# One opening block instead of two, and another order at the borders of two attentions

## What is computed

```python
x = x + L0_xattn(layernorm(x), ctx, mask)   # 16 heads of 128, 8 key/value heads
x = x + L0_ffn(layernorm(x))                # weights rounded to fp8, silu(gate) * up
x = x + L1_xattn(layernorm(x), ctx)         # 16 heads, queries and keys RMS-normed per head
x = x + L1_ffn(layernorm(x))                # 16 experts, top 2
# xattn: q = xn @ Wq, k = ctx @ Wk, v = ctx @ Wv, softmax(q k / sqrt(128)) v, @ Wo
# RMS norm of q and k: t * rsqrt(mean(t^2) + eps) * g
```

## Time and profile before

| | |
|---|---|
| median of 3 runs | 2272.78 us (2270.73 to 2275.41) |
| the profiled execution | 2273.29 us, span 2271.6 us |
| busy over the span | PE 94%, DVE 68%, ACT 56%, POOL 25% |
| stages in the span, about | opening to 37 us, attention 0 to 766, ffn 0 to 1052, attention 1 to 1946, experts after it |

### The profile page before, as it was taken

One profiled execution on the slowest core, in us unless ns is written; L12 is line 12 of the kernel. 1 busy time (PEld: TensorE's weight loads), 2 busy tenths in 40 slices (PEclk: granted clock), 3 DMA queues, 4 the chain that ended last, 5 costly groups with the idle time before them and its releaser, 6 DMA issues. The chain is left out here.

```text
span 2271.6 us, 38211 instructions
## 1 busy us (share of the span) xinstructions
PE 2137.9 (94%) x12318; PEld 1864.9 (82%) x12318; DVE 1554.3 (68%) x3798; ACT 1260.9 (56%) x3373; POOL 560.4 (25%) x1274
## 2 busy tenths in 40 slices
PE   5999999999999899998999999999999999589993
PEld 4899999999999678887788888888888888378882
DVE  6777777777778884434666666666666667867776
ACT  4555455455454533323666666666666666567772
POOL 1000001001000122223333333333333333144541
PEclk8999999999999999999999999999999999789997
DMA  6122111111210220002111111111111110278886
GB/s 254 65 80 80 46 69 63 61 69 46 78 57 27 70 75 1 1 1 75 47 56 47 56 63 57 46 55 46 55 46 55 58 55 36 83 246 293 291 277 259
DMA packets 74388, 195.83 MB, mean 86 GB/s; under 512 B 8448, under 2 KB 39192, under 8 KB 61488
## 3 DMA queue, kind: packets, MB, share of 16 engines
q1 hardware_dynamic: 64432, 173.60, 21.9%
q0 software_dynamic: 7680, 16.80, 2.2%
q10 hardware_dynamic: 2176, 4.19, 0.5%
HBM read 177.78 MB, written 25.17 MB: 89 GB/s over the span
## 5 line engine op out<-in xcount | busy, mean ns | idle before, releaser
L608 PE MATMUL bank<-l_wkv_hi,l_ctxT 128*128 128x256 f32 (+1 forms) x1024 | 278.8, 344 | 7.0 <-DMA l_ctxT<-ctx_split 5.2
L1025 DVE TENSOR_TENSOR l_v_lo<-bank,l_v_hi 128x128 fp32r<-128x128 f32 (+1 forms) x256 | 91.7, 358 | 213.5 <-ACT l_v_hi L847 212.2
L1025 DVE TENSOR_TENSOR l_pT_lo<-bank,l_pT_hi 128x512 fp32r<-128x512 f32 x256 | 175.2, 684 | 77.9 <-ACT l_pT_hi L872 77.9
L866 ACT ACTIVATE l_probs<-l_scored,l_nbias 128x256 f32<-128x256 f32 x256 | 128.2, 502 | 158.6 <-DVE l_nbias L1078 155.6
L608 PE MATMUL bank<-l_wo_hi,l_oT_hi 128*128 128x512 f32 x512 | 209.3, 409 | 0.7 <-DVE l_oT_lo L1025 0.7
L608 PE MATMUL bank<-xnT_hi,l_wq_hi 128*128 128x512 f32 x512 | 209.8, 410 | 0.0
L608 PEld LDWEIGHTS bank<-l_wkv_hi,l_ctxT 128*128 128x128 f32 x1024 | 183.3, 193 | 28.2 <-issue 6.3
L608 PE MATMUL bank<-xnT_lo,l_wq_hi 128*128 128x512 f32 x512 | 201.7, 394 | 0.0
L608 PE MATMUL bank<-xnT_hi,l_wq_lo 128*128 128x512 f32 x512 | 201.7, 394 | 0.0
L608 PE MATMUL bank<-l_wo_hi,l_oT_lo 128*128 128x512 f32 x512 | 201.1, 393 | 0.0
L608 PE MATMUL bank<-l_wo_lo,l_oT_hi 128*128 128x512 f32 x512 | 200.8, 392 | 0.0
(11 more groups left out here) (288 smaller groups left out, 5949.9 us busy)
## 6 DMA issues: line engine op xcount, KB each, us to landing
l_ctxT<-ctx_split SPq DMA_DIRECT2D x64, 1024.0 KB, 4.8
moe_raw_gu<-in_L_ffn_gate_up_proj SPq DMA_DIRECT2D x32, 1024.0 KB
moe_raw_dn<-in_L_ffn_down_proj SPq DMA_DIRECT2D x32, 512.0 KB
l_raw_a<-in_L_xattn_Wq SPq DMA_DIRECT2D x16, 512.0 KB, 5.8
l_raw_a<-in_L_xattn_Wo SPq DMA_DIRECT2D x16, 512.0 KB, 5.4
x_sb<-in_x SPq DMA_DIRECT2D x4, 1024.0 KB, 11.1
ctx_split<-ct SPq DMA_DIRECT2D x4, 1024.0 KB, 13.6
moe_raw_gu<-moe_y_rows SPq DMA_DIRECT2D x4, 1024.0 KB
```

Of the source, the lines that this page charges most:

```text
L608: mm = nc.tensor.matmul(out, a[x], b[y], start=(i == 0), stop=(i == n - 1))
L866: ins = nc.scalar.activation(probs[u % 2][:, t, :], src, ACT.Exp, bias=nbias[:, i:i + 1], scale=scale, accum_out=rsum[:, i:i + 1])
L1025: nc.vector.tensor_tensor(pair[1], src, pair[0].bitcast(F32), ALU.subtract).then_inc(done, 1)
```

## The change

**Opening.** The two stages become one block, `opening_stage`. DMA order: x group 0, x group 1, both context halves, the weights, x groups 2 and 3. DVE does the layer norm factors of 8 tiles before it touches the context. The normalised rows come from three engines (DVE 1, ACT 4, POOL 3), rows and context groups alternate on PE, ACT and DVE, and rows use four banks in turn. Group 0 of the split context is written straight into `ctxT`, and SP raises `ctx_in` itself, so group 0 isn't loaded back; groups 1 to 3 are kept in parts of `xnT` that are free until later. All four are still stored. In attention 0, SP waits for the four stores before it loads group 1, and ACT before its first `turned_high`.

**Attention borders.** In layer 1's prologue DVE scales the first keys and POOL takes the first query factors; DVE waits for them before the first `biases`. In layer 1's first iteration `split_o` and `split_p` (unit 2) go ahead of `biases` (unit 3). In the last iteration of both layers `copy_p` and `split_p` of unit 0 go ahead of the exponentials of unit 1 and of `statistics`. At the end of layer 1 the statistics of the third group move from the last but one iteration into the last, `take_sums` goes first on DVE, `norm_queries` comes before `late_factors(1)` on POOL, and `normalise(4, 5)` moves behind the exponentials of unit 2.

```diff
+            load_x(0)
+            load_x(1)
+            load_c(0)
+            load_c(1)
             ahead.sync(sp)
             load_x(2)
             load_x(3)
             for g in range(NG):
                 sp.wait_ge(c_lo, KC * (g + 1))
...
+            sp.sem_inc(ahead.ctx_in, 16)
...
+            pool.wait_ge(chain, CHAIN)
+            for t in POOL_TILES:
+                apart(k, pool)
+                gp.tensor_scalar(xn[t][:, :], k.x_sb[:, t, :], rstd[:, t:t + 1], shift[:, t:t + 1], ALU.mult, ALU.add).then_inc(pool_normed, 1)
+            ahead.gpsimd(pool)
...
+            for g in range(2):
+                turn_c(g)
+            for t in range(4):
+                turn_row(t)
+            turn_c(2)
+            for t in (4, 5):
+                turn_row(t)
+            turn_c(3)
+            for t in (6, 7):
+                turn_row(t)
...
+            for g in range(2):
+                context_high(g)
+            act.wait_ge(chain, CHAIN)
+            normalise(1)
+            normalise(3)
+            row_high(0)
+            row_high(1)
+            normalise(5)
+            row_high(2)
+            row_high(3)
+            normalise(6)
+            context_high(2)
+            row_high(4)
+            row_high(5)
+            ahead.scalar(act)
+            context_high(3)
+            row_high(6)
+            row_high(7)
...
+            for g in range(2):
+                context_low(g)
+            for t in range(4):
+                row_low(t)
+            context_low(2)
+            for t in (4, 5):
+                row_low(t)
             dve.wait_ge(k.x_in[2], 32)
+            for t in range(TILES, TILES + TG):
+                next_statistics(t)
+            context_low(3)
+            for t in (6, 7):
+                row_low(t)
...
@@ attention, SP
+                sp.wait_ge(k.ctx_stored, 16 * NG)
             sp.wait_ge(kv_made, TG)
             load_ctx(sp, 1)
@@ attention, POOL
             if rms:
                 norm_keys(*PROLOGUE, first=True)
+                first_query_factors()
             ln_group_factors(first_tiles, N1)
...
                     if rms:
                         norm_queries(hg, g)
+                    if rms and ending(hg, g):
+                        late_factors(1)
...
-                    if ending(hg, g + 1):
+                    if ending(hg, g + 1) and not rms:
                         late_factors(1)
@@ attention, ACT
+                act.wait_ge(k.ctx_stored, 16 * NG)
                 turned_high(0, 1)
...
+                    if ending(hg, g):
+                        copy_p(hg, g, 0)
                     exponentials(hg, g, 1)
...
-                            late(normalise, 4, 5)
...
                         if rms:
+                            late(normalise, 4, 5)
                             late(turned_high, 2, 3)
@@ attention, DVE
+            def scale_first_keys():
+                dve.wait_ge(k_chain, 1 + RSQRT_STEPS)
...
+                nc.vector.tensor_tensor(kn3, kn3, scale, ALU.mult).then_inc(k_ready, 1)
...
+                scale_first_keys()
+                take_sums(0, 0, 0)
+                dve.sem_inc(q_ready, 1)
                 first_moments()
-                take_sums(0, 0, 0)
-                first_query_factors()
...
+            if rms:
+                dve.wait_ge(den_chain, 1 + RSQRT_STEPS)
             biases(0, 0, 0)
...
+                    if rms and ending(hg, g):
+                        take_sums(hg, g, 1)
                     if rms:
                         denominators(hg, g, 0)
                     biases(hg, g, 1)
                     if not opening(hg, g):
                         split_o(hg, g - 1, 1)
+                    if not rms and ending(hg, g):
+                        split_p(hg, g, 0)
...
+                    if rms and ending(hg, g):
+                        statistics(hg, g - 1, (2, ))
+                        split_p(hg, g, 0)
+                        statistics(hg, g - 1, (3, ))
+                        denominators(hg, g, 1)
+                        moments(hg, g - 1)
+                        low_late(0, 1)
...
+                    if rms and opening(hg, g):
+                        split_o(hg, g, 0)
+                        split_p(hg, g, 2)
                     biases(hg, g, 3)
...
+                    if rms and ending(hg, g + 1):
+                        biases(hg, g + 1, 0)
                     split_q(hg, g, 1)
+                    if rms and ending(hg, g + 1):
+                        statistics(hg, g, (1, ))
```

More of the change, by code:

```diff
@@ L145, in layernorm_stage @@
[L145 to L171, removed]
-        @block.gpsimd
-        def _(pool):
-            ahead.gpsimd(pool)
-        @block.vector
-        def _(dve):
-            done = [TG]
@@ L181, in step @@
+            done = [0]
             def step(ins, wait=True):
@@ L207, in _ @@
-        @block.tensor
-        def _(pe):
-            for t in range(TILES):
-                wait_normed(pe, t)
-                for c in range(KD):
-                    mm = nc.tensor.transpose(banks[t][:, P * c:P * (c + 1)], xn[t][:, P * c:P * (c + 1)], k.ident[:, :])
-                mm.then_inc(turned, 1)
-        @block.scalar
-        def _(act):
-            def normalise(t):
-                nc.scalar.activation(xn[t][:, :], k.x_sb[:, t, :], ACT.Identity, bias=shift[:, t:t + 1],
-                                     scale=rstd[:, t:t + 1]).then_inc(act_normed, 1)
-            ahead.scalar(act)
-            act.wait_ge(chain, CHAIN)
-            later = list(ACT_TILES)
-            for t in range(TILES):
-                while later and later[0] <= t + 3:
-                    normalise(later.pop(0))
-                act.wait_ge(turned, t + 1)
-                nc.scalar.copy(k.xnT_hi[:, :, P * t:P * (t + 1)], banks[t][:, :].rearrange("p (k t) -> p k t", k=KD)).then_inc(hi_done, 1)
+                                        ALU.subtract, ALU.mult).then_inc(dve_normed, 1)
@@ L945, in iteration @@
                     if rms:
-                        copy_p(hg, g, 0)
+                        if not ending(hg, g):
+                            copy_p(hg, g, 0)
                         if opening(hg, g):
@@ L1219, in iteration @@
                         denominators(hg, g, 1)
-                        split_p(hg, g, 0)
+                        if not ending(hg, g):
+                            split_p(hg, g, 0)
                         split_q(hg, g, 0)
@@ L1259, in iteration @@
                         denominators(hg, g, 3)
-                    split_o(hg, g, 0)
-                    split_p(hg, g, 2)
+                    if not rms or not opening(hg, g):
+                        split_o(hg, g, 0)
+                        split_p(hg, g, 2)
                     if not opening(hg, g):
@@ L1289, in iteration @@
                             split_k(hg, g, h)
-                        if not ending(hg, g):
+                        if not ending(hg, g) and not ending(hg, g + 1):
                             statistics(hg, g, (1, 2, 3))
@@ L2424, in decoder_layers @@
             start = attention_start(k, ahead, "l0", *w0[:3], rms=False)
[L2425 to L2428 removed]
+            waiting = [xnT[:, :, GT * g:GT * (g + 1)].rearrange("p (a k) t -> p a k t", a=2)
+                       for xnT, g in ((k.xnT_hi, 2), (k.xnT_lo, 3), (k.xnT_hi, 3))]
+            k.ct = [start.ctxT[:, :, :, :]] + waiting
+            opening_stage(k, x, ctx_1024, start)
             attention_stage(k, "l0", start, w0[3], mask=mask, following=ffn, early=FIRST, early_rows=ffn.rows, rounds=ffn)
```

126 lines of the change are left out of this document (75 added, 51 removed).

## The result

| | before | after | ratio, 95% interval |
|---|---|---|---|
| median, first set of runs | 2272.71 us (2270.73 to 2275.41) | 2260.65 us (2259.55 to 2262.47) | 0.9946 (0.9936 to 0.9956) |
| median, second set (`after_again`) | 2273.36 us | 2262.63 us (2261.42 to 2263.86) | 0.9952 (0.9938 to 0.9966) |
| the profiled execution | 2273.29, span 2271.6 | 2261.2, span 2259.4 | |

The change makes the kernel 12.1 us faster in one set of runs and 10.7 in the other (0.9946 and 0.9952 of about 2273 are 12.3 and 10.9). The forecast was 9.9 faster, 2262.9.

The account below looks back on a forecast made before the run. PE, busy 94% of the span, was taken as the bound, with only its idle time at the borders to win. -6.8 + 0 - 1.6 + 0 - 1.5 = -9.9 gave 2262.9 us; own range 2260 to 2266, eight in ten 2257 to 2268.

Parts of the forecast that it names:

- Opening, -6.8: Opening block: PE starts at 30.3 us and wins 7.0, of which 0.2 is given back to DVE's statistics.
- rival B: Opening: POOL takes its three rows first and DVE's row waits 3.8 us; opening gives 4.0, total 2265.7; chance 0.06.
- the two parts: Opening: the reload of context group 0, priced at 2.4 us, and the late layer norm, at 4.6.
- New waits, 0: After the opening: SP's and ACT's waits for the stores cost 0, covered by about 1.5 us for SP.
- Rival D: Opening: the last of the four stores lands late and holds ACT; a landing at 60 gives 2279; chance 0.03.
- End of attention 0, 0: `weigh_v` starts about 1.7 us earlier, but PE meets the same stop behind POOL: 0, bounds 0 and -1.7.
- Start of attention 1, -1.6: Key scaling on DVE, query factors on POOL: first scores at 1070.25 instead of 1071.86 us; bounds -0.7 to -2.2.
- Split ahead of bias, 0: Attention 1's first iteration: unit 2's wait shrinks by 1.4 us, the next transposes wait instead; net 0 (-0.7 to +0.3).
- End of attention 1, -1.5: PE's wait for POOL's query factors goes; unit 3's division, transposes and `weigh_v` follow 1.5 us earlier; bounds -0.5 to -2.5.
- Rival C: Less idle time in the opening, at 741 and at 1913 spares half-clock stretches, 4 us more: 2258.9; chance 0.13.
- Rival E: Opening: ACT's 23 instructions are slower, the block still ends near 34.4, only the reload is saved: 2267.3; chance 0.08.
- Rival A: Only the opening pays; attention 1's border gains run into the next POOL chain: 2266.0; chance 0.15.

Follow-up runs that it names:

- after_again: The kernel after, unchanged, timed and profiled a second time: 2262.63 us, 0.9952 of before.
- opening_only: The kernel before with only the new opening block and the two waits on the stores: 2266.77 us, 0.9970 of before.
- context_first: The kernel after with the DMA order of before (context half, x group, context half, x group): 2267.75 us, 0.9973 of before.
- reload_group0: The kernel after, but SP waits for all four stores and loads group 0 of the split context back: 2271.29 us, 0.9986 of before.
- bias_first_hold: As bias_first, but POOL's scaling of the second group's keys waits until unit 3's bias is done: 2260.77 us, 0.9936 of before.
- statistics_out: The kernel after with x group 2's four statistics moved from the opening block to attention 0's start: 2261.62 us, 0.9947 of before.
- bias_first: The kernel after with unit 3's bias ahead of split_o and split_p again in attention 1's first iteration: 2261.12 us, 0.9943 of before.
- borders_only: The kernel before with only the new orders at the borders of the two attentions: 2269.61 us, 0.9981 of before.

## Why the prediction was right

- **Opening, -6.8.** Right in size: -7.4 in the trace, 6.8 by the ratio of `opening_only`. Factors were forecast at 15.3 and came at 15.66, DVE's end at 29.6 and 29.48, PE at 30.3 and 29.95. POOL's rows took 0.84 each, under the bound of 0.95, and DVE's row 0.55 beside them: rival B (POOL first) didn't happen. Of the 0.2 given back behind the start, at most 0.1 shows (-7.39 at the first product, -7.33 at the first scores, 51.98 and 44.65). What failed is that the two parts add up: the reload's 2.4 is borne out by the 2.1 of `context_first`, but `reload_group0` shows that the layer norm's 4.6 don't pay while the reload stands (-0.5).
- **New waits, 0.** Right: the first product of attention 0 and the first of attention 1 moved by the same 7.4 to 7.5. The last store was issued at 28.32, and SP issued the load of group 1 at 35.73, where the key/value tiles let it (forecast 35.6). Rival D is out.
- **End of attention 0, 0.** Right by the step named: the gain of 1.6 runs into POOL's chain. In size it was -0.1 in five traces and +0.8 in six, which the bounds of 0 and -1.7 don't hold.
- **Start of attention 1, -1.6.** The mechanism is right and the first scores came 1.93 earlier: 0.73 of it by the keys, as forecast. What became of it behind the scores wasn't in the sum. There the profiled execution gained 1.5 more, by a clock that stayed at 2.4 GHz at 1084 to 1096 us, and `after_again` gave 1.7 back; the other six traces with these orders gave back 0.2 to 2.1. The undone prologue costs 2.0 us by the ratios (0.9958 against 0.9949, the mean of the two sets of after), with an uncertainty as large, and nothing by its trace.
- **Split ahead of bias, 0.** This is the term that was mis-sized. The shift from the wait for unit 2 to the next transposes happened: that wait is new and 1.84 us long, which the prediction had named as a sign of being wrong (a new wait of PE of over 1 us in the borders). 1.0 us of what the order won was DVE held by POOL, which the forecast didn't have. From unit 2 to the next scores PE took 0.5 us more than before in the first profile, and 2.5 to 3.1 more in the other seven.
- **End of attention 1, -1.5.** Right: -1.43 in the first profile, -1.24 in the second, and PE's wait for POOL is gone as forecast. This is the border whose gain is in nearly every trace.
- **Sum.** The terms as the first trace has them are -7.4, -0.1, -3.7 and -1.4, with 0.4 given back behind the last projection. As the second has them they are -7.5, +0.4, -0.5 and -1.2, with 0.6 more behind it. The forecast of -9.9 lies between -9.5 and -12.2. That it does so is in part luck: the end of attention 0 and the start of attention 1 did worse than forecast in most traces, and the medians (10.7 and 12.1) are better than those traces would give. Rival C, 4 us more by the clock, was this mechanism in the wrong place. From 12 to 80 us the mean clock rose from 0.82 to 0.87 and 0.90, so of these 68 us some 24 were at 1.2 GHz before and 18 and 14 after (twice the missing share), but little of PE's work lay in them: between the first product and 720 us the two executions gained 0.0 and 0.4. What the clock did change fell at 740 and 1090 us. Rival E is out by PE's start. Rival A is out by the end of attention 1, where no POOL chain took the gain; at the start little was left in seven of eight traces, but for the clock and not for POOL.

Why the gain by the medians is 0.8 to 2.2 us above the forecast isn't fully settled: the part of the clock in each run's time can't be read without its trace, and two profiles of one kernel differ by 2.7.

## What to carry to other kernels

Before the parts of a fix are priced one by one, ask whether two chains end at the same wait: here the early layer norm gave nothing while the reload stood, the kept tile gave 2.1 us without the new DMA order, and together they gave 7.4. A microsecond won behind a short idle stretch of PE is worth what the clock leaves of it, so a border is judged from several executions, not from one profile. A tiny VectorE instruction on a critical path should not be due while GpSimd runs a long one (both read SBUF here): put it ahead and let GpSimd wait, which took 1.0 us off the wait in `bias_first_hold` and cost nothing that the trace shows.

## What the runs showed of the hardware

- A DVE instruction of 128x2 elements took 1.17 us beside a POOL instruction of 128x1024 that had started first, up to 1.94 us elsewhere, and 0.16 alone; where it was looked at, it ended when POOL's did.
- One kernel, profiled twice, had a granted clock of 1.00 and of 0.72 in the same 12 us of its work, with equal waits of PE there (1.05 and 1.84 us). Its two spans were 2259.4 and 2262.1 us. At the end of attention 0 eleven traces with the same order fell into two groups, 27.8 and 28.7 us, at a mean clock of 1.00 (after, `statistics_out`) and of 0.81 or 0.82 (`after_again`, `bias_first`, `borders_only`, `reload_group0`) over 18 us.
- 1 MB stored to DRAM was free to be loaded back 5.1 us after the store was issued, and the load back took 4.9 (`reload_group0`).
- The same scaling of 128x1024 elements took 1.89 us on POOL and 1.22 on DVE.
